# Graph attention on one core: the order of four engines' work inside a step, and the banks for turned rows

## What is computed

```python
h = _layer_norm(x, g1, b1)
q = (h @ Wq + bq).reshape(n, NH, HD)          # 8 heads of 16
k = (h @ Wk + bk).reshape(n, NH, HD)
s_all = jnp.concatenate([src, loops])
d_all = jnp.concatenate([dst, loops])
e = jnp.sum(q[d_all] * k[s_all], axis=-1) / np.sqrt(HD)
```

## Time and profile before

| | us |
|---|---|
| median of 3 runs (lowest, highest) | 2435.67 (2431.19, 2440.10) |
| the profiled execution: its time, its span | 2436.44, 2434.7 |
| of the span: from the first gather of `attention` (1044.24) to the end of its last copy of logits (1334.74) | 290.5 |

### The profile page before, as it was taken

How to read it: one execution, slowest core, us unless ns; L and a number is a source line. 1 busy time by engine, 2 the same in 40 slices (tenths; PEclk the granted TensorE clock), 3 DMA queues, 4 the chain that set the end, 5 groups by cost and what they waited for, 6 DMA issues and landing times. The chain is left out here.

```text
span 2434.7 us, 49516 instructions
## 1 busy us (share of the span) xinstructions
PE 2066.7 (85%) x14383; PEld 1685.0 (69%) x14383; DVE 1912.1 (79%) x7786; ACT 1330.5 (55%) x3176; POOL 1228.3 (50%) x1418
## 2 busy tenths in 40 slices
PE   3777777759997888849999399992999999999998
PEld 2555555559997888737776289881777777777776
DVE  3999999978885889869997877773777777777774
ACT  1899999933332455568886200001556666566665
POOL 2764444247772777667772157775333333333332
PEclk9999999989998999979999699996999999999999
DMA  3888888779997688655552156664133333333321
GB/s 85 259 259 242 243 244 241 212 216 292 295 287 242 197 231 237 185 153 164 162 161 75 48 144 195 202 200 152 54 110 111 105 105 105 109 110 108 105 96 53
DMA packets 353686, 413.33 MB, mean 170 GB/s; under 512 B 51340, under 2 KB 235040, under 8 KB 353418
## 3 DMA queue, kind: packets, MB, share of 16 engines
q1 hardware_dynamic: 315850, 339.88, 44.3%
q0 software_dynamic: 34496, 69.37, 11.4%
q10 hardware_dynamic: 3072, 0.92, 0.2%
HBM read 263.50 MB, written 179.89 MB: 182 GB/s over the span
## 5 line engine op out<-in xcount | busy, mean ns | idle before, releaser
L1807 PEld LDWEIGHTS p_y<-w,g_T 128*128 128x128 f32 x3136 | 365.4, 192 | 46.4 <-issue 24.2
L1807 PE MATMUL p_y<-w,g_T 128*128 128x128 f32 x3136 | 365.8, 275 | 0.0
L1825 ACT ACTIVATE nT<-p_n 128x512 f32<-128x512 f32 x98 | 58.5, 597 | 560.3 <-PE p_n L1815 560.3
L1800 PE MATMUL p_f<-nT,w 128*128 128x512 f32 x784 | 354.0, 594 | 0.0
L1790 POOL TENSOR_TENSOR rstd<-var,minus_half 128x4 f32<-128x4 f32 x98 | 113.8, 1161 | 450.3 <-ACT res L1838 450.1
L547 POOL DMA_INDIRECT x_dst<-in_x_dram,idx x196 | 192.2, 981 | 226.9 <-DMA edge_x<-x_dst 144.3
L1832 ACT ACTIVATE g_T<-p_f,bf 128x512 f32<-128x512 f32 x392 | 266.7, 680 | 31.1 <-PE p_f L1800 31.0
L901 POOL DMA_INDIRECT h_src<-h_table,idx x196 | 189.5, 967 | 104.1 <-issue 58.6
L1800 PEld LDWEIGHTS p_f<-nT,w 128*128 128x128 f32 x784 | 141.9, 191 | 141.4 <-issue 141.4
L1597 POOL DMA_INDIRECT x_rows<-xv,idx x196 | 195.6, 998 | 77.8 <-issue 55.2
L1130 POOL DMA_INDIRECT x_src<-x_rows,idx x196 | 184.9, 943 | 85.4 <-issue 55.5
(11 more groups left out here) (321 smaller groups left out, 5548.6 us busy)
## 6 DMA issues: line engine op xcount, KB each, us to landing
xs<-x_rows SPq DMA_DIRECT2D x98, 512.0 KB, 3.7
x_in<-in_x_dram SPq DMA_DIRECT2D x98, 256.0 KB, 4.1
h_table<-h_rows SPq DMA_DIRECT2D x98, 256.0 KB
x_rows<-x_in SPq DMA_DIRECT2D x98, 256.0 KB, 2.9
out_dram<-res SPq DMA_DIRECT2D x98, 256.0 KB, 2.1
x_rows<-x_rows SPq DMA_DIRECT2D x50, 500.0 KB
edge_x<-x_dst SPq DMA_DIRECT2D x98, 128.0 KB, 2.6
h_own<-edge_x SPq DMA_DIRECT2D x49, 256.0 KB, 6.2
```

The source lines that it names most:

```text
L1800: e.matmul(p_f[ch][:], w_1[:, ch * P:(ch + 1) * P], nT[:, g % 2, :], start=True, stop=True).then_inc(f_prod, 1)
L1807: mm = e.matmul(p_y[g % 2][:, a * D:(a + 1) * D], g_T[:, g % 2, ch, a * P:(a + 1) * P], w_2[:, ch, :], start=(ch == 0), stop=(ch == FCH - 1))
```

## The change

The groups, the tiles and every operation with its operands stay as they are. What changes is the lag of the pieces, their order on each engine, and some rings:

- Lags: statistics 3; `std` 4; reciprocal, `shift`, both normalisations 5 (`NORM`); turning 6 (`TURN`); `srcT` and `carry` 7 (`CARRY`); the three matmuls 8 (`PROD`); `qT` and `prod` 9; head sums 10 (`SUM`); copy of the logits 11. The loop has 61 steps in place of 58.
- Order in ACT's step: copy of logits, `qT`, `srcT`, normalise destinations, `std`, normalise sources.
- Order in DVE's step: destination statistics, carry 3, product s, carry 2, product d, carry 1, reciprocal, carry 0, kept, source statistics, `shift`, eight `bn_aggr`.
- Order in PE's step: turn destinations, turn sources, head sums, q, ks, kd.
- `p_src` and `p_dst` get two banks each (all 8 banks are then used); rings: `x_src` and `x_dst` 7 groups, `rows` 8, `mv` 4. SP asks for `x_dst` before `rows`.

Core of the diff (the bodies of pieces that are only moved are left out):

```diff
-            SN, ON = 6, 4
+            SN, RN, ON = 7, 8, 4
...
-                p_dst, p_src, p_q, p_kd, p_ks, p_sum = (ps(name, c) for name in ("p_dst", "p_src", "p_q", "p_kd", "p_ks", "p_sum"))
+                p_src = [ps(f"p_src{s}", c) for s in range(2)]
+                p_dst = [ps(f"p_dst{s}", c) for s in range(2)]
...
+                NORM = AHEAD + 2
+                TURN = NORM + 1
+                CARRY = TURN + 1
+                PROD = CARRY + 1
+                SUM = PROD + 2
+                STEPS = GE + SUM + 2
...
                 @block.tensor
+                        if at_step(n, TURN):
+                            e.wait_ge(dst_normed, k + 1)
+                            wait(e, dstT_ready, GT * (k - 1))
...
+                            e.wait_ge(src_normed, k + 1)
+                            wait(e, srcT_ready, k - 1)
...
+                        if at_step(n, SUM):
+                            e.wait_ge(prod_s_ready, k + 1)
+                            e.wait_ge(prod_d_ready, k + 1)
+                            wait(e, logit_ready, k)
...
-                        if at_step(n, AHEAD + 3):
+                        if at_step(n, PROD):
...
                 @block.scalar
-                        if at_step(n, AHEAD + 5):
+                        if at_step(n, SUM + 1):
                             e.wait_ge(summed, k + 1)
...
+                        if at_step(n, PROD + 1):
+                            e.wait_ge(q_prod, k + 1)
...
+                        if at_step(n, CARRY):
                             e.wait_ge(src_turned, k + 1)
...
-                        if at_step(n, AHEAD + 1):
+                        if at_step(n, NORM):
                             e.wait_ge(shift_ready, k + 1)
...
                         if at_step(n, AHEAD + 1):
+                            e.wait_ge(mv_ready, k + 1)
...
+                        if at_step(n, NORM):
                             wait(e, src_turned, k - 1)
...
                 @block.vector
+                        if at_step(n, AHEAD):
+                            row_stats(k, 0)
+                        if at_step(n, CARRY):
+                            carry(n - CARRY, 3)
+                        if at_step(n, PROD + 1):
+                            logit_terms(n - PROD - 1, 1, p_ks, ks_prod, prod_s_ready)
+                        if at_step(n, CARRY):
+                            carry(n - CARRY, 2)
+                        if at_step(n, PROD + 1):
+                            logit_terms(n - PROD - 1, 0, p_kd, kd_prod, prod_d_ready)
+                        if at_step(n, CARRY):
+                            carry(n - CARRY, 1)
+                        if at_step(n, NORM):
+                            e.wait_ge(std_ready, k + 1)
...
+                        if at_step(n, CARRY):
+                            carry(n - CARRY, 0)
```

More of the change, by code:

```diff
@@ L1078, in attention @@
                 stats = sb("stats", [P, 2, 2 * GT, 6], F32, c)
[L1079 removed]
+                mv = sb("mv", [P, 4, 2 * GT, 2], F32, c)
                 std = sb("std", [P, 2, 2 * GT], F32, c)
@@ L1123, in _ @@
                 def _(e):
[L1124 to L1132, removed]
+                    for k in range(GE):
+                        wait(e, src_normed, k - SN + 1)
+                        for j in range(GT):
+                            t = group(k) * GT + j
+                            e.indirect_dma_start(out=x_src[:, k % SN, j, :], out_offset=None, in_=x_rows,
+                                                 in_offset=bass.IndirectOffsetOnAxis(ap=idx[:, X_SRC, t:t + 1], axis=0))\
+                                .then_inc(gathered[k % SN], 16)
                 @block.sync
@@ L1147, in _ @@
                                 .then_inc(dst_in[k % SN], 16)
+                            wait(e, dstT_ready, GT * (k - RN + 1))
+                            e.dma_start(rows[:, k % RN, :, :], edge_row(group(k), TO_NEXT, TO_NEXT + 1)).then_inc(rows_in[k % RN], 16)
                     for k in range(ON):
@@ L1175, in _ @@
                             e.matmul(p_kd[:], w_vqk[:, 2 * D:3 * D], dstT[:, k % ON, :], start=True, stop=True).then_inc(kd_prod, 1)
[L1176 to L1186, removed]
                 @block.scalar
@@ L1195, in _ @@
                                          p_sum[:, 0:GT * 2 * HEADS], ACT.Copy).then_inc(logit_ready, 1)
-                        if at_step(n, AHEAD + 2):
-                            k = n - AHEAD - 2
+                        if at_step(n, PROD + 1):
+                            k = n - PROD - 1
+                            e.wait_ge(q_prod, k + 1)
+                            wait(e, prod_s_ready, k - 1)
+                            wait(e, prod_d_ready, k - 1)
+                            e.activation(qT[:, k % 2, :], p_q[:], ACT.Identity, bias=bias_vqk[:, 1:2]).then_inc(qT_ready, 1)
+                        if at_step(n, CARRY):
+                            k = n - CARRY
                             e.wait_ge(src_turned, k + 1)
-                            e.activation(srcT[:, group(k), :], p_src[:], ACT.Copy).then_inc(srcT_ready, 1)
-                        if at_step(n, AHEAD + 1):
-                            k = n - AHEAD - 1
+                            e.activation(srcT[:, group(k), :], p_src[k % 2][:], ACT.Copy).then_inc(srcT_ready, 1)
+                        if at_step(n, NORM):
+                            k = n - NORM
                             e.wait_ge(shift_ready, k + 1)
@@ L1207, in _ @@
                             ins.then_inc(dst_normed, 1)
[L1208 to L1213, removed]
                         if at_step(n, AHEAD + 1):
                             k = n - AHEAD - 1
+                            e.wait_ge(mv_ready, k + 1)
+                            wait(e, rstd_ready, k - 1)
+                            e.activation(std[:, k % 2, :], mv[:, k % 4, :, 1], ACT.Sqrt, bias=eps[:]).then_inc(std_ready, 1)
+                        if at_step(n, NORM):
+                            k = n - NORM
                             wait(e, src_turned, k - 1)
@@ L1220, in _ @@
                             ins.then_inc(src_normed, 1)
[L1221 to L1225, removed]
                 @block.vector
@@ L1249, in row_stats, with logit_terms @@
                         ins.then_inc(stats_ready, 1)
-                    for n in range(STEPS):
-                        if at_step(n, AHEAD + 1):
-                            k = n - AHEAD - 1
+                    def logit_terms(k, a, p_k, made, done):
+                        e.wait_ge(qT_ready, k + 1)
+                        wait(e, summed, k - 1)
+                        e.wait_ge(made, k + 1)
+                        e.scalar_tensor_tensor(out=prod[:, k % 2, a, :], in0=p_k[:], scalar=bias_vqk[:, 2:3],
+                                               in1=qT[:, k % 2, :], op0=ALU.add, op1=ALU.mult).then_inc(done, 1)
+                    for n in range(STEPS):
+                        if at_step(n, AHEAD):
+                            k = n - AHEAD
+                            e.wait_ge(dst_in[k % SN], 16 * (k // SN + 1))
+                            wait(e, mv_ready, k - 1)
+                            row_stats(k, 0)
[10 more added lines that the diff above has]
+                        if at_step(n, NORM):
+                            k = n - NORM
                             t = group(k) * GT
@@ L1265, in _ @@
+                        if at_step(n, NORM):
+                            k = n - NORM
                             e.wait_ge(rstd_ready, k + 1)
                             e.tensor_tensor(rstd[:, k % 2, 0:GT], rstd[:, k % 2, 0:GT], done_col[:, t:t + GT], ALU.mult).then_inc(kept_ready, 1)
-                        if at_step(n, AHEAD + 2):
-                            carry(n - AHEAD - 2, 3)
-                        if at_step(n, AHEAD + 1):
+                        if at_step(n, AHEAD):
+                            k = n - AHEAD
+                            e.wait_ge(gathered[k % SN], gathered.after(k % SN, GT * (k // SN + 1)))
+                            row_stats(k, 1)
@@ L1273, in _ @@
                         if at_step(n, AHEAD):
[L1274 to L1288, removed]
-                            ins.then_inc(mv_ready, 1)
[L1290 to L1295, removed]
-                            for a, p_k, made, done in ((1, p_ks, ks_prod, prod_s_ready), (0, p_kd, kd_prod, prod_d_ready)):
-                                e.wait_ge(made, k + 1)
-                                e.scalar_tensor_tensor(out=prod[:, k % 2, a, :], in0=p_k[:], scalar=bias_vqk[:, 2:3],
-                                                       in1=qT[:, k % 2, :], op0=ALU.add, op1=ALU.mult).then_inc(done, 1)
+                            k = n - AHEAD
@@ L1301, in softmax @@
+                            e.wait_ge(stats_ready, 2 * (k + 1))
+                            wait(e, shift_ready, k - 3)
+                            for j in range(2 * GT):
```

(2 more changed lines are left out.)

54 lines of the change are left out of this document (25 added, 29 removed).

## The result

The changed kernel took 2535.93 us as the median of 4 runs (2532.11 to 2537.53), the kernel before 2435.82 (4 runs): a ratio of 1.041, 95% interval 1.039 to 1.043. In the profiled executions it is 2536.74 against 2436.44, + 100.3. All of it lies in `attention`: from its first gather (1043.2) to the end of its last copy of logits (1433.8) it lasts 390.6 us, where it was 290.5, + 100.1.

What follows compares the result with a forecast made beforehand. PE's work (5.35 us a step) and a ring through ACT and DVE (5.40) were read as level bounds. + 99.4 to the last `shift` and + 5.0 behind it make + 104.4 on 2435.67: 2540 us, range 2526 to 2572.

Steps and rivals of the forecast that it cites:

- The ring: In `attention`, DVE's product, `shift`, ACT's normalisation, `qT` and the next product wait in a circle, one turn per step.
- Its length: One turn through DVE (3.93 us) and ACT (3.62): a step of 7.55 in place of 5.40, bounds 7.4 to 7.9.
- The start: Fill of `attention` up to the `shift` of step 9, put at 1087.4 us, give or take 4.
- the old ring: Kernel before: `std`, reciprocal, `shift`, normalisation, `qT` and back to `std` through ACT and DVE, 5.40 us a step.
- Up to then gathers and normalisations pace the fill as they do now: Before step 9, filling keeps its pace: sixth group's source statistics at 1079.1 us, 5.40 before the seventh's.
- The end: Behind the last `shift` PE sets the pace: 21.3 us where it was 16.3, so + 5.0.
- The banks, gathers, SP's order: Second PSUM banks worth 0; POOL's gathers, 4.9 us, fit under 7.55; SP's store wait stands ahead of loads as before.
- The clock rival: TensorE's clock falls with PE's gaps; at a mean of 0.65 the step is 8.23, time 2570; chance 0.12.
- PE about 71% busy: Sign that the forecast is right: PE busy 5.35 of each 7.55 us step in `attention`.
- The 2679: Time in us if transposes don't count as busy and half clock makes the step 10.7 us.
- The rival without a ring: PE's 5.35 us alone binds `attention`: 2436 to 2444, say 2438; no change 0.04, faster 0.01.
- 5.35 is a floor for any order: PE's busy time in one `attention` step, 5.35 us, claimed as the least step that any order allows.

Runs made afterwards that it cites:

- e1: Changed kernel with reciprocal, kept and `shift` moved to the front of DVE's step, ahead of both products: ratio 0.9991 to the kernel before.
- e6: Changed kernel with both normalisations one step after `shift`, all behind them one step later, gather rings 8, flags 9: ratio 1.0003 to the kernel before.
- e2: Changed kernel with `shift` alone moved ahead of the four source statistics in DVE's step: 2505.1 us, one run.
- e4: Kernel before with only two banks each for the turned rows and PE's two waits a group looser: ratio 0.9996.
- e8: Kernel before with destination statistics moved from between reciprocal and kept to behind `shift` in DVE's step: ratio 0.9993.
- e9: Kernel before with both destination statistics and carry 3 moved behind `shift` in DVE's step: ratio 0.9942.
- e3: Changed kernel with each group's kd matmul made twice into the same bank: 2541.1 us, one run.
- e5: Kernel before with head sums alone moved behind turning and ahead of q in PE's step: 2475.0 us, one run.

## Why the prediction was right, point by point

The forecast was 2540 with + 104.4; measured are 2535.9 and + 100.1 to 100.3.

- **The ring**, the step on which all rests: right. It shows in the waits, e1 and e6 cut it in two ways, and e2 shortens it by what was taken out of it.
- **Its length**: 7.45 for 7.55. Three terms were a little long: copy of logits to `qT` 0.10 (taken as 0.15, with 0.11 as the lower bound), carry to carry 0.47 (0.49), kept to statistics 0.07 (0.10); the others are off by 0.01 or so, some up, some down. From the `shift` of step 9 to the last one it was 326.6 us for 330.5.
- **The start**: the `shift` of step 9 came at 1083.3, not 1087.4. I had let the fill run at the 5.40 of the old ring, but in the new order it went at the pace of the gathers: the sixth group's source statistics came at 1075.1 after a wait for its gather (1.65 us), for 1079.1. The step of the prediction that failed here is "Up to then gathers and normalisations pace the fill as they do now": before, the statistics of the second to the tenth group wait for no gather at all.
- **The end**: 24.0 us behind the last `shift`, for 21.3. The clock was 0.86 there, and PE turned the last group at 1414.53 only, 1.3 us behind ACT. The last head sums took 2.44 us for 1.85. So the clock cost some 2 us in all, at the one place where PE sets the pace. Counted from the first gather, which itself came 1.1 us earlier than in the kernel before, - 3.1 for the start, - 3.9 for the ring and + 2.7 for the end make the 4.3 us between 104.4 and 100.1.
- **The banks, gathers, SP's order**: nothing, as said; for the banks e4 shows it in the old order, the others are seen only in that no wait of the ring goes to them (POOL's waits for the normalisation are those of an engine that is ahead).
- **The clock rival**: the clock fell, to a mean of 0.83 with a dip in nearly every second step, but not to the 0.65 that the rival needs: 5.35 / 0.83 = 6.4 is under 7.45. The sign "PE about 71% busy" failed: PE reads 92% (36.80 of 40), by the lower clock and by matmul ends that are modelled; e2, at a clock of 1.00, also reads 33.25 of 40, where 5.24 of 6.80 us would be 30.8. That transposes don't count as busy for the clock (the Trainium skill, TensorE: Matmul & The Clock Gate, Part 4) no run here shows or excludes. The 2679 that the prediction worked out from it did not come, and the working was wrong in itself: the rule takes out the turning alone, and the head sums, 1.89 us a step, are matmuls like q, ks and kd.
- **The rival without a ring**: its time, 2436 to 2444, is about what e1 and e6 took (2435.8, 2437.9), but by luck, as two errors cancel: PE's step is 5.24, not 5.35, which saves more than the 2 us of the rival, and the end is 11 us longer, not 2 to 10 for start and end together.
- **"5.35 is a floor for any order"**: wrong, and the worst step of the text, though it cost nothing here. PE's busy time includes up to 0.18 us a step in which the last matmul's modelled end covers a wait for the normalisation. So before the change the kernel was bound by two rings through ACT, not by PE.

## What to carry to other kernels

Write for each pair of engines which hand-overs lie in the same step and in which direction they go; wherever two go in opposite directions, add up start to start from one to the other and back, and compare with the step. Either remedy is cheap: let each engine do what the other waits for before it waits itself, or give one of the two a step of its own. And when one ring is cut and the step doesn't move, look for a second that was level with it: here the first of two cuts was worth nothing alone (e8), and both together 0.6% (e9).

## What the runs showed of the hardware that I had not expected

- TensorE's clock went between its two levels from step to step for 326 us, at a mean of 0.85, with 7.45 us a step; with 6.80 us (e2) and an idle gap of 1.1 us in each step it stayed at 1.00 from 1116 to 1295, and with 5.40 too. With more matmul work in the same 7.45 us (e3) it was 0.96 in the window 1200 to 1240. The length of the step doesn't decide it alone: with 6.05 us and another order of PE (e5) it dipped, to a mean of 0.95 from 1116 to 1295.
- A PE busy 39.63 of 40 us had 0.2 us to give in each step of 5.40 us (e9, with the same order on PE, takes 5.19): 16 matmuls of 8 columns and the next start are 1.71 apart when nothing is waited for, and 1.89 in the kernel before, with the same 1.85 of busy time.
